# Four PSUM banks for the spreads of three attention stages, and heads that compact all chunks first

## The reference

```
x = x + 0.5 * ffn(layernorm(x))
x = x + attention(layernorm(x))
x = x + 0.5 * ffn(layernorm(x))
```

## Time and profile before

| | us |
|---|---|
| median of three timed runs | 3961.26 (3960.78 to 3961.97) |
| the profiled execution | 3964.23 |
| its span | 3962.4 |
| TensorE busy | 3388.7 |
| VectorE busy | 2717.1 |
| ScalarE busy | 1863.8 |
| POOL busy | 970.9 |

### The profile page before, as it was taken

How to read it: one execution, slowest core, us unless ns; L and a number is a source line. 1 busy time by engine, 2 the same in 40 slices (tenths; PEclk the granted TensorE clock), 3 DMA queues, 4 the chain that set the end, 5 groups by cost and what they waited for, 6 DMA issues and landing times.

```text
span 3962.4 us, 55781 instructions
## 1 busy us (share of the span) xinstructions
PE 3388.7 (86%) x21909; PEld 1719.3 (43%) x21909; DVE 2717.1 (69%) x5772; ACT 1863.8 (47%) x3334; POOL 970.9 (25%) x772
## 2 busy tenths in 40 slices
PE   3679875799975999999979998988998888899899
PEld 2322222465641233333346565656674222323576
DVE  7787778777754999999657785364434777776433
ACT  1232221477742577777757774313221256666321
POOL 0235551477720000000057771000201101111100
PEclk8878977799985899999989998979998688889899
DMA  0000000211100000000021110000200000000100
GB/s 20 9 0 0 0 0 0 71 29 36 29 6 0 1 1 1 1 1 1 1 72 29 36 29 24 6 23 19 71 1 27 0 1 1 1 1 1 44 1 11
DMA packets 48255, 60.16 MB, mean 15 GB/s; under 512 B 9268, under 2 KB 34232, under 8 KB 47608
## 3 DMA queue, kind: packets, MB, share of 16 engines
q1 hardware_dynamic: 47992, 56.59, 5.2%
HBM read 39.22 MB, written 1.10 MB: 10 GB/s over the span
## 4 chain that ended last, share of the span: by engine, by line


## 5 line engine op out<-in xcount | busy, mean ns | idle before, releaser
L142 PE MATMUL ps<-AR 128*128 128x128 f32 (+9 forms) x16848 | 2174.9, 437 | 217.8 <-DVE AR L122 74.4
L131 ACT ACTIVATE AR<-ps 128x1024 f32<-128x1024 f32 (+6 forms) x1768 | 1277.1, 762 | 1130.8 <-PE ps L142 855.7
L142 PEld LDWEIGHTS ps<-AR 128*128 128x128 f32 (+5 forms) x16848 | 1030.7, 152 | 1396.8 <-issue 403.3
L125 DVE TENSOR_REDUCE AR<-ps 128x1 f32<-128x512 f32 (+1 forms) x1424 | 936.6, 709 | 155.3 <-PE ps L142 154.8
L114 POOL TENSOR_TENSOR AR<-AR 128x512 f32<-128x512 f32 (+4 forms) x422 | 549.6, 1315 | 851.4 <-ACT AR L131 570.7
L131 ACT ACTIVATE AR<-ps,AR 128x128 f32<-128x128 f32 (+1 forms) x764 | 402.4, 544 | 457.8 <-PE ps L142 430.0
L114 POOL TENSOR_TENSOR rs<-rs,halves 128x4 f32<-128x4 f32 x68 | 71.1, 1046 | 1915.5 <-DVE rs L118 1914.7
L142 PE MATMUL ps<-XT,AR 128*128 128x512 f32 x896 | 437.3, 624 | 6.9 <-DMA AR<-in_L3a_bvo 3.2
L114 DVE TENSOR_TENSOR AR<-ps,AR 128x512 f32<-128x512 f32 (+3 forms) x626 | 300.8, 529 | 136.0 <-PE ps L142 99.1
L122 DVE SCALAR_TENSOR_TENSOR X<-ps,AR,X 128x128 f32<-128x128 f32 x512 | 143.8, 344 | 345.7 <-PE ps L142 345.3
L150 PE MATMUL ps<-C,AR 128*128 128x128 f32 x1593 | 250.6, 295 | 135.0 <-ACT AR L131 61.0
(11 more groups left out here) (84 smaller groups left out, 1857.2 us busy)
## 6 DMA issues: line engine op xcount, KB each, us to landing
AR<-AR SPq DMA_DIRECT2D x124, 128.0 KB, 2.3
AR<-in_c_rot SPq DMA_DIRECT2D x64, 128.0 KB, 2.3
AR<-in_L3f_w SPq DMA_DIRECT2D x32, 256.0 KB, 5.9
AR<-in_L2f_w SPq DMA_DIRECT2D x32, 128.0 KB, 2.6
AR<-scr_bias SPq DMA_DIRECT2D x32, 128.0 KB, 3.2
WR<-in_c_rot SPq DMA_DIRECT2D x1, 2048.0 KB, 8.9
WR<-in_L_ffn_wqkv SPq DMA_DIRECT2D x2, 768.0 KB
AR<-in_L_ffn_wqkv SPq DMA_DIRECT2D x2, 768.0 KB
```

The costliest lines, as they stand in the source:

```text
L125: return self.do(lambda e: e.tensor_reduce(o, a, AXX, op, negate=neg, apply_absolute_value=mag), *w)
L131: return self.do(lambda e: e.activation(o, a, f, bias=bias, scale=scale, accum_out=acc), *w)
L142: last = e.matmul(o, l, r, start=a, stop=z, skip_group_check=True)
```

## The change

`spread` of `l0_attn` takes four banks in turn (5, 6, 0, 1) for the chunks 2 and 3. In `attn8`, both cases now prepare all chunks first: all turns, then chunk by chunk the compaction (banks 0 to 3) and the spread of group 0 (banks 6 and 5), k before q. While the head lasts (`in_head`), items that spread take the banks 0 to 3 in turn and not one of the ring of three. In the causal case `background` now holds value rows 0 to 7, the key spreads of group 1, value rows 8 to 15 and the query spreads of group 1.

```diff
         def spread(j):
-            b = 5 + j % 2
+            b = (5, 6, 0, 1)[j % (2 if c < 2 else 4)]
...
-    tT = {} if causal else dict(enumerate(turn(g, g.XN, g.XT, tn)))
-
-    def turn_in(c, b):
-        t = P.tr([(g.bank[b][:, 128 * k:128 * k + 128], g.XN[:, 4 * c + k, :]) for k in range(4)],
-                 g.ident, g.free[b], tn[4 * c:4 * c + 4])
-        g.free[b] = tT[c] = A.act(g.XT[:, 512 * c:512 * c + 512], g.bank[b], ACT.Copy, t)
+    tT = turn(g, g.XN, g.XT, tn)
...
-    def compact(c, k, b, b2):
+    def compact(c, k):
+        b, b2 = 2 * k, 2 * k + 1
...
+    in_head, nsp = [False], [0]
...
     def spread_step(gr, c, k):
-        return lambda: later.append(spread(gr, c, k, spare()))
+        def step():
+            nsp[0] += 1
+            later.append(spread(gr, c, k, nsp[0] % 4 if in_head[0] else spare()))
+        return step
...
-    def chunk_steps(c, banks):
-        def some(k):
-            return banks[k] if banks else spare()
-        return [lambda: turn_in(c, some(0)), lambda: compact(c, 1, some(1), some(2)), lambda: compact(c, 0, some(3), some(0))]
...
+    for c in range(5):
+        if c >= 1:
+            for k in (1, 0):
+                later.append(spread(0, c - 1, k, 5 + k))
+        if c < 4:
+            for k in (1, 0):
+                compact(c, k)
+        flush()
+    in_head[0] = True
     if causal:
-        for step in chunk_steps(0, (0, 1, 2, 3)):
-            step()
-        background.extend(spread_step(0, 0, k) for k in (1, 0))
-        for c in range(1, 4):
-            background.extend(chunk_steps(c, None))
-            background.extend(spread_step(0, c, k) for k in (1, 0))
-            background.extend(value_rows(i) for i in range(4 * c - 4, 4 * c))
-        background.extend(value_rows(i) for i in range(12, 16))
+        background.extend(value_rows(i) for i in range(8))
         background.extend(spread_step(1, c, 1) for c in range(4))
+        background.extend(value_rows(i) for i in range(8, 16))
         background.extend(spread_step(1, c, 0) for c in (3, 2, 1, 0))
     else:
-        for c in range(5):
-            if c >= 1:
-                for k in range(2):
-                    later.append(spread(0, c - 1, k, 5 + k))
-            if c < 4:
-                for k in range(2):
-                    compact(c, k, 2 * k, None)
-            flush()
         for i in range(NT):
             project_v(i)
...
     while rows_due:
         max_rows(rows_due.pop(0))
+    in_head[0] = False
```

## The result

The kernel after takes 3869.95 us (median of four runs, 3867.59 to 3874.09) where the kernel before took 3961.33 us beside it: a ratio of 0.977, with an interval of 0.9753 to 0.9787. That is 91.4 us less. The forecast was 3889 us; the time lies at the lower end of the range (3870), 0.05 us outside it. Direction and mechanism were right, and all three terms of the sum were too small. The profiled execution of the kernel after took 3874.09 us with a span of 3872.3 us, so the spans differ by 90.1 us.

What follows compares the result with a forecast made beforehand. It took a bank-reuse latency loop in `l1_attn`'s head, blocks of idle VectorE in `l3_attn` and bank waits in the first attention as bounds; -56.5 - 13 - 2.5 = -72 us from 3961.3 gave 3889 us, range 3870 to 3914.

Steps and rivals of the forecast that it cites:

- The ring: `l1_attn` head: three spare banks, three requests per half iteration, so each spread waits for the previous spread's low part; 4.65 us.
- I take 2.25 us, near the middle: `l1_attn` head: new half iteration put between 1.95 and 2.62 us; 24 take 54 us for 110.5, so -56.5 us.
- The lower bound of 1.95: `l1_attn` head: shortest half iteration, VectorE the bound at the upper clock, 1.21 us maxima plus 0.74 us low part.
- The loop of before agrees with that: `l1_attn` head: old loop's 2.03 us idle at clock 0.50 to 0.52 said to fit a clock dropping again and again.
- For the cost of one more chunk I take the chain: `l3_attn` head: products, VectorE, POOL and spread added up, 7.9 us a chunk at upper clock, 11.8 at lower.
- I take 8.5: `l3_attn` head: us per further chunk; three add 25.5 us, within a first step +14 us later and -13 us net.
- rival 5: `l3_attn` steps without holes run at a higher clock: another 15 to 25 us, 3869 us or less; chance 0.08.
- TensorE is itself busy in 30.4 of 33 us, so not all can go: First attention, chunk 3: only part of 4.5 us VectorE idle time goes; -2.5 us, bounds 0 and -4.5.
- The clock that stays low (1): `l1_attn` new loop stays at the lower clock, half iteration 2.62 us, kernel 3898 us; chance 0.20.
- nothing from the serial head (2): `l3_attn` head: chunks cost 11.8 us each with nothing beside them, no gain, kernel 3902 us; chance 0.14.
- an unbroken loop (3): `l1_attn` head: something else at the same pace holds the spreads, loop not broken, kernel 3946 us; chance 0.05.
- slower steps (4): `l3_attn`: 160 steps wait for a slower bank reader, 0.6 us each, kernel 3985 us; chance 0.03.

Runs made afterwards that it cites:

- e1: Kernel before, with only the spreads in the head of `l1_attn` on banks 0 to 3: 3890.85 us, ratio 0.9829.
- e4: Kernel after, but the spreads in both heads use bank 0 alone: 3929.12 us, ratio 0.9922.
- e6: Kernel after, with 20 scratch fills on VectorE ahead of the `l1_attn` loop while TensorE stands still: `l1_attn` 830.00 us.
- e3: Kernel before, with only the four banks in the first attention: 3953.11 us, ratio 0.9985.
- e2: Kernel after with only the causal attention's part kept, the other two parts undone: 3940.89 us, ratio 0.9953.
- e5: Kernel after, but the spreads in both heads use banks 0 and 1 in turn: 3874.18 us in one run.
- e12: Kernel after, unchanged, run again beside others on one chip: 3870.52 us, ratio 0.9781.
- e11: Kernel after, with chunk 3 of `l3_attn` moved from the head into the background list: 3874.4 us, ratio 0.9788.
- e7: Kernel after, with all sixteen value rows ahead of the group 1 key spreads in the causal background list: 3877.53 us in one run.
- e8: Kernel after, with the rotation tables loaded ahead of the six weight loads of `l3_attn`: 3870.73 us, ratio 0.9778.
- e13: The same kernel as e10 a second time, beside e12: 3863.67 us, ratio 0.976.
- e10: Kernel after, with `l3_attn` rotation tables loaded ahead of the weights and `l0_attn` probabilities turned through two banks: 3870.93 us, ratio 0.9774.

## Why the prediction was right, and where its sizes were off

**Head of `l1_attn`: -56.5 forecast, -63.0 measured.** The ring, its cause and its way out were as read from the earlier trace rows; e1 and e4 show them one by one. The step that was mis-sized is "I take 2.25 us, near the middle". Measured are 46.4 us / 24 = 1.93 us a half iteration, with VectorE as the limit. The lower bound of 1.95 wasn't quite one: in the steady loop a low part takes up 0.66 us of VectorE's time, not the 0.74 of its row, and the period is 1.855. The middle between two levels of a clock was a poor choice: this loop runs at one level or at the other, and e6 shows how both look (2.54 and 1.855 us), and that it leaves the lower one after 12.3 us. Of the two rows that I weighed, the maxima-only one at 0.50 spoke for a loop that isn't like this one. "The loop of before agrees with that" was a misreading: its clock was low, but it fell once and didn't drop again and again (windows beside e6).

**Head of `l3_attn`: -13 forecast, -22.1 measured.** Over more profiles the figure holds: the old head took 677.88, 673.45 and 676.38 us (before, e1, e3; mean 675.9), the new one 652.15 to 656.24 us in six (after, e2, e4, e5, e6, e12; mean 654.9), 21.0 less. Its parts:
- The first scores: +14 forecast, +9.1 measured (+10.6 between the means of three profiles with the old head and six with the new one). Most of the miss is "For the cost of one more chunk I take the chain" and "I take 8.5". The three further chunks took 8.99, 6.92 and 6.92 us, 22.8 and not 25.5, and two of them lie under my lower bound of 7.9. The end of the last chunk, up to the maxima, took 4.3 us and not 5.8, the maxima loop with its tail 12.7 and not 14; the wait for the tables was 0.4 us longer. The chain itself was another one. The timeline of VectorE beside the spreads at 2985.30 and 2992.22:

```profile
2988.18 3.33 DVE L122 SCALAR_TENSOR_TENSOR AR<-ps,AR,WR 128x512 f32<-128x512 f32 x4 [2.28 <-PE ps L142]
2991.43 1.40 DVE L122 SCALAR_TENSOR_TENSOR AR<-AR,ps 128x512 bf16<-128x512 bf16 x2
```

TensorE makes the second pair of products while VectorE rotates the first, and the sum on POOL is done (2991.21) before the next spread starts. That spread waits 1.50 us for L122, the low part of the chunk before on its own bank, which stands in VectorE's queue behind the four rotations: 1.82 us for two spreads, 1.06 for the first products, 3.25 for the rotations and 0.79 for the low part are the 6.92. It is the same kind of wait as the one that was broken in `l1_attn`; other banks for these spreads were not tried.
- What comes back: 26.5 forecast; 26.0 measured up to `finish` 2 (27.4 between the means). This is the best hit of the prediction, and e11 shows with 13.7 us for chunk 3 that the chunks' blocks are its main part. That the forced spreads bring 3 of it was not tested; e7 could not bring them back.
- A further 5.0 us came behind `finish` 2, where the work is the same. That was rival 5, put at 15 to 25 us. It is the granted clock (0.92 for 0.87), and it isn't stable. From `finish` 2 to the end of the stage the three profiles with the old head take 463.5 to 464.6 us, the six with the new one 458.9 to 461.3 (means 4.2 us apart), but e7, e8 and e13, with the same instructions there, 462.5 to 467.3 and e10 456.7. Whether the new head favours the good phase is open.

**First attention: -2.5 forecast, -4.9 measured** (466.27 to 467.02 without the banks, 461.17 to 461.90 with them, nine profiles), beyond the bound of -4.5. The wrong step is "TensorE is itself busy in 30.4 of 33 us, so not all can go". All of the 0.26 us waits went. The 44 weightings of chunk 3 gave 4.3 us of this in the profile after and 5.4 in e3. The idle time of 4.5 us was no bound, because a part of the weightings took 0.60 us each afterwards and not 0.6475. TensorE's busy time in the earlier trace rows wasn't its need: from 574.5 to 603.1 it made 69 products in 26.15 us before (0.38 us each, clock 0.88) and 80 in 27.30 us after (0.34 us each, clock 0.94).

**Rivals.** The clock that stays low (1), nothing from the serial head (2), an unbroken loop (3) and slower steps (4) did not come. The time lies 19 us under the forecast, in the 15 to 25 of rival 5 (though 1 us above its 3869 us), but it got there by another way: three terms at or past their good ends, -6.5, -9.1 and -2.4 us beside the forecast, and only 5 us of that by rival 5's mechanism. The range was built from the sum of all bounds, 90 us, and the three stages came to 90.0, so no room was left. That this sum just held is partly luck: the time of 1.95 us a half iteration, the 7.9 us a chunk and the idle time of chunk 3 were passed, and none of them was a true bound.

**The signs.** Seen in `l1_attn` were the 46.4 us for 24 spreads (47 to 63 expected), TensorE's own wait for L122 gone and VectorE busy in 99% of it. In `l3_attn` the first scores came 8.7 us later after the table load than before (42.8 and 34.1 us) and not 12 to 20, and in chunk 3 of the first attention 28.3 us passed and not 28.5 to 33. "I am wrong if one of the two heads comes out of its bounds": `l1_attn` kept to them with -63.0, and `l3_attn` stands at their edge, with -22.1 for "about -22" (-21.0 over the profiles).

## What to carry to other kernels

When a loop asks for as many buffers per turn as its ring holds, each user meets its own last reader; look for a period in which no engine is full, and count requests per turn before counting buffers. Of private banks for the slow user one gave nothing (865.06 us), two gave all (802.19), four no more (802.38). A forecast for a loop that can run at two clock levels should be one of the two ends, and the row that decides it must come from a loop with the same mix of work. Preparation that is scattered into a tight steady loop cost 13.7 us a piece here and 8.3 us ahead of it, together with its like (e11), so where such pieces overlap with each other, try them together, ahead.

## What the runs showed of the hardware that was not expected

Two stretches of `l1_attn` after, one behind the other, both have TensorE busy in 93% (43.28 of 46.4 us, 17.55 of 18.8) and VectorE full; the one with float32 spreads among the maxima is at a clock of 0.99 and the one with maxima alone at 0.50, as before. So the busy share in the profile alone doesn't tell the clock; which property of the mix does was not tested.

Stages with the same instructions in two executions differ by some us (`l0_ffn2` 110.59 to 113.55, `l1_ffn` 418.86 to 422.25, `l1_ffn2` 415.94 to 419.80, `l2_attn` 66.78 to 69.43), and `l3_attn` of one and the same program took 655.82 and 652.15 us, and of another (e10, e13) 649.05 and 655.96. This is as large as the smaller edits here, so a stage's length from one profile is good to about 4 us, and in `l3_attn` to 7. The 63.0 us of `l1_attn` are far beyond that, and the 21 us of `l3_attn` stand on nine profiles.
